# GroupNorm and self-attention block: rows of x load into the result's buffer, GpSimd adds the bias, and plain stores replace copies and accumulation

## The reference

```python
def _gn(v, G=32, eps=1e-5):
    g = v.reshape(B_, H_, W_, G, C_ // G)
    m = jnp.mean(g, axis=(1, 2, 4), keepdims=True)
    s = jnp.var(g, axis=(1, 2, 4), keepdims=True)
    return ((g - m) / jnp.sqrt(s + eps)).reshape(v.shape)

# inside _L0_conv_ref(inputs, Wq, bq, ...)
q = x @ Wq + bq
k = x @ Wk + bk
v = x @ Wv + bv
scores = jnp.einsum('bnc,bmc->bnm', q, k) * scale
attn = jax.nn.softmax(scores, axis=-1)
attended = jnp.einsum('bnm,bmc->bnc', attn, v)
out = attended @ Wo + bo

x = x + _L0_conv_ref(_gn(x), Wq, bq, Wk, bk, Wv, bv, Wo, bo)
```

## Time and profile before

| | before |
|---|---|
| median of three runs | 1805.6 us (1804.97 to 1805.94) |
| the profiled execution's own time | 1804.94 us |
| its span | 1803.3 us |
| TensorE (PE) busy | 1796.9 us, 100% |
| VectorE (DVE) busy | 1633.2 us, 91% |
| ScalarE (ACT) busy | 1056.0 us, 59% |
| GpSimd (POOL) busy | 91.1 us, 5% |
| DMA | 101.92 MB, mean 57 GB/s |
| granted TensorE clock | full, in every slice |

### The profile page before, as it was taken

How to read it: one execution, slowest core, us unless ns; L and a number is a source line. 1 busy time by engine, 2 the same in 40 slices (tenths; PEclk the granted TensorE clock), 3 DMA queues, 4 the chain that set the end, 5 groups by cost and what they waited for, 6 DMA issues and landing times.

```text
span 1803.3 us, 32710 instructions
## 1 busy us (share of the span) xinstructions
PE 1796.9 (100%) x11589; PEld 1642.3 (91%) x11589; DVE 1633.2 (91%) x2860; ACT 1056.0 (59%) x1417; POOL 91.1 (5%) x106
## 2 busy tenths in 40 slices
PE   9999999999999999999999999999999999999999
PEld 8989999899898999998999989999899898999989
DVE  7999899999998999989999999899998998999997
ACT  5565565665655656556565565565665656656563
POOL 0000000000000000000000000000000000000000
PEclk9999999999999999999999999999999999999999
DMA  3222122231222221322213232122221222311201
GB/s 117 59 70 66 23 62 58 70 70 37 44 60 68 70 52 29 69 59 70 58 23 70 58 70 63 21 67 58 70 70 34 47 59 69 70 47 34 68 14 36
DMA packets 28809, 101.92 MB, mean 57 GB/s; under 512 B 3189, under 2 KB 3962, under 8 KB 28794
## 3 DMA queue, kind: packets, MB, share of 16 engines
q0 software_dynamic: 9072, 33.03, 12.1%
q1 hardware_dynamic: 19722, 68.69, 11.4%
HBM read 68.16 MB, written 66.58 MB: 75 GB/s over the span
## 4 chain that ended last, share of the span: by engine, by line
PE 96%; DVE 2%; issue 1%; ACT 0%; POOL 0%; POOLq 0%; DVEq 0%; ACTq 0%
PE ps_s L861 47%; PE ps_o L955 13%; PE ps_o L956 13%; PE ps_o L957 13%; PE ps_o L861 9%; DVE s_buf L627 1%; PE ps_o L965 0%; DVE top L597 0%; DVE o_buf L647 0%; DVE query_max L614 0%; DVE h_lo L569 0%; ACT s_buf L347 0%; DVE top_turned L602 0%; DVE part_max L604 0%; DVE row_max L620 0%
## 5 line engine op out<-in xcount | busy, mean ns | idle before, releaser
L955 PE MATMUL ps_o<-v_rows,p_hi 128*128 128x258 f32 x2048 | 577.9, 282 | 0.0
L957 PE MATMUL ps_o<-v_rows,p_lo 128*128 128x258 f32 x2048 | 576.1, 281 | 0.0
L956 PE MATMUL ps_o<-v_lo,p_hi 128*128 128x256 f32 x2048 | 575.8, 281 | 0.0
L355 ACT ACTIVATE p_hi<-s_buf 128x1024 fp32r<-128x1024 f32 x256 | 272.3, 1064 | 439.1 <-DVE s_buf L627 439.1
L861 PE MATMUL ps_s<-g_hi,h_hi 128*128 128x512 f32 x1024 | 399.5, 390 | 1.1 <-DVE g_lo L577 0.9
L861 PE MATMUL ps_s<-g_hi,h_lo 128*128 128x512 f32 x1024 | 399.0, 390 | 0.0
L861 PE MATMUL ps_s<-g_lo,h_hi 128*128 128x512 f32 x1024 | 398.6, 389 | 0.0
L955 PEld LDWEIGHTS ps_o<-v_rows,p_hi 128*128 128x128 f32 x2048 | 385.9, 188 | 2.4
L956 PEld LDWEIGHTS ps_o<-v_lo,p_hi 128*128 128x128 f32 x2048 | 384.8, 188 | 2.9
L957 PEld LDWEIGHTS ps_o<-v_rows,p_lo 128*128 128x128 f32 x2048 | 384.6, 188 | 0.0
L347 ACT ACTIVATE s_buf<-ps_s 128x512 f32<-128x512 f32 x512 | 292.4, 605 | 136.3 <-PE ps_s L861 134.7
(11 more groups left out here) (95 smaller groups left out, 2229.3 us busy)
## 6 DMA issues: line engine op xcount, KB each, us to landing
x_t<-in_x_turned_dram SPq DMA_DIRECT2D x64, 512.0 KB, 3.9
out_dram<-in_x_dram SPq DMA_DIRECT2D x63, 512.0 KB, 7.1
out_dram<-o_buf POOLq DMA_DIRECT2D x63, 512.0 KB, 5.4
x_last<-in_x_dram SPq DMA_DIRECT2D x1, 512.0 KB, 7.6
out_dram<-o_buf SPq DMA_DIRECT2D x4, 128.0 KB, 2.0
s_buf<-in_L_conv_Wq_dram SPq DMA_DIRECT2D x1, 256.0 KB, 5.1
s_buf<-in_L_conv_Wk_dram SPq DMA_DIRECT2D x1, 256.0 KB, 5.3
s_buf<-in_L_conv_Wv_dram SPq DMA_DIRECT2D x1, 256.0 KB, 5.5
```

Of the source, the lines that this page charges most:

```text
L355: nc.scalar.activation(p_hi[c][:, rows, :], s_buf[c][:, rows, :], ACT.Exp, scale=SCALE).then_inc(p_hi_done, 1)
L955: nc.tensor.matmul(ps[:, 0:VC], p_hi[c][:, m, cols], v_hi[:, m, :], start=m == 0, stop=False)
L956: nc.tensor.matmul(ps[:, VC - C:VC], p_hi[c][:, m, cols], v_lo[:, m, :], start=False, stop=False)
L957: last = nc.tensor.matmul(ps[:, 0:VC], p_lo[c][:, m, cols], v_hi[:, m, :], start=False, stop=m == T - 1)
```

## The change

The rows of x are no longer copied from DRAM to DRAM. For each image and half they load into o_buf[c] itself. GpSimd adds out_bias to them in place, an instruction over 128x1024 with two inputs in SBUF. finish then adds the attend to what stands in o_buf[c], tile by tile, and SyncE stores the buffer with a plain transfer. As load and result share a buffer, a load waits for the store before it (stored), GpSimd for the load (rows_in), VectorE's first finish for GpSimd (rows_biased), and the store for the four finishes (o_out). The last image does the same, apart from the tile-by-tile stores at its end, which stay; x_last goes. weighed has a buffer of its own.

```diff
-        x_last = sb("x_last", [P, TQ, C])
+        weighed = sb("weighed", [P, C])[:]
...
-            def residual(b, c):
-
-                after(sp, x_copied[c], b * 16)
-                sp.dma_start(out_v[b, :, c * TQ:(c + 1) * TQ, :],
-                             x_v[b, :, c * TQ:(c + 1) * TQ, :]).then_inc(x_copied[c], 16)
+            def load_rows(b, c):
+                after(sp, stored[c], b * 16)
+                sp.dma_start(o_buf[c][:], x_v[b, :, c * TQ:(c + 1) * TQ, :]).then_inc(rows_in[c], 16)
+
+            def store(b, c):
+                sp.wait_ge(o_out, b * 8 + (4 * c + 4))
+                sp.dma_start(out_v[b, :, c * TQ:(c + 1) * TQ, :], o_buf[c][:]).then_inc(stored[c], 16)
...
             load_turned(1)
-            residual(0, 0)
-            residual(0, 1)
-            residual(1, 0)
-            residual(1, 1)
+            load_rows(0, 0)
+            load_rows(0, 1)
 
             def body(b):
                 load_turned(b + 1)
-                residual(b + 1, 0)
-                residual(b + 1, 1)
+                store(b - 1, 0)
+                load_rows(b, 0)
+                store(b - 1, 1)
+                load_rows(b, 1)
...
-            with sp.Fori(1, B - 2) as b:
+            with sp.Fori(1, B - 1) as b:
                 body(b)
-            load_turned(B - 1)
-            residual(B - 1, 0)
-            sp.dma_start(x_last[:], x_v[B - 1, :, TQ:2 * TQ, :]).then_inc(x_last_in, 16)
+            store(B - 2, 0)
+            load_rows(B - 1, 0)
+            store(B - 2, 1)
+            load_rows(B - 1, 1)
+            store(B - 1, 0)
             store_last_tiles()
...
-            def store(b, c):
-
-                after(pool, x_copied[c], b * 16 + 16)
-                after(pool, o_out, b * 8 + (4 * c + 4))
-                pool.dma_start(out_v[b, :, c * TQ:(c + 1) * TQ, :], o_buf[c][:],
-                               accum_op=ALU.add).then_inc(stored[c], 16)
+            def add_bias(b, c):
+                pool.wait_ge(rows_in[c], b * 16 + 16)
+                pool.tensor_tensor(o_buf[c][:], o_buf[c][:], out_bias[:].unsqueeze(1).broadcast_to([P, TQ, C]),
+                                   ALU.add).then_inc(rows_biased[c], 1)
...
             inverse_std(0)
             inverse_std(1)
-            store(0, 0)
+            pool.wait_ge(out_bias_done, 1)
+            add_bias(0, 0)
+            add_bias(0, 1)
             with pool.Fori(1, B - 1) as b:
-                store(b - 1, 1)
+                add_bias(b, 0)
                 inverse_std(b + 1)
-                store(b, 0)
-            store(B - 2, 1)
-            store(B - 1, 0)
+                add_bias(b, 1)
+            add_bias(B - 1, 0)
+            add_bias(B - 1, 1)
...
                 if j == 0:
-                    dve.wait_ge(out_bias_done, 1)
-                    after(dve, stored[c], b * 16)
+                    dve.wait_ge(rows_biased[c], b + 1)
...
-                                               in1=out_bias[:] if rows is None else rows, op0=ALU.mult, op1=ALU.add).then_inc(o_out, 1)
+                                               in1=o_buf[c][:, j, :], op0=ALU.mult, op1=ALU.add).then_inc(o_out, 1)
...
-                dve.wait_ge(x_last_in, 16)
-                nc.vector.tensor_tensor(x_last[:], x_last[:], out_bias[:].unsqueeze(1).broadcast_to([P, TQ, C]),
-                                        ALU.add).then_inc(x_last_done, 1)
```

More of the change, by code:

```diff
@@ L146, in attention_kernel @@
         bias_rows = tail[0:2 * K, 8 + C:8 + C + P]
-        weighed = o_buf[1][:, 0, :]
         wq_in = sem("wq_in")
@@ L154, in attention_kernel @@
         bias_turned = sem("bias_turned")
-        x_last_in = sem("x_last_in")
-        x_last_done = sem("x_last_done")
+        rows_in = [sem(f"rows_in{c}") for c in range(CH)]
+        rows_biased = [sem(f"rows_biased{c}") for c in range(CH)]
         last_stored = sem("last_stored")
@@ L168, in attention_kernel @@
         fold_done = sem("fold_done")
-        x_copied = [sem(f"x_copied{c}") for c in range(CH)]
         xt_landed = [sem(f"xt_landed{k}") for k in range(K)]
@@ L262, in store_last_tiles @@
                                  o_buf[1][:, j:j + 1, :]).then_inc(last_stored, 16)
-            with sp.Fori(1, B - 2) as b:
+            with sp.Fori(1, B - 1) as b:
                 body(b)
-            load_turned(B - 1)
-            residual(B - 1, 0)
-            sp.dma_start(x_last[:], x_v[B - 1, :, TQ:2 * TQ, :]).then_inc(x_last_in, 16)
+            store(B - 2, 0)
[3 more added lines that the diff above has]
+            store(B - 1, 0)
             store_last_tiles()
-            after(sp, x_copied[0], 16 * B)
-            after(sp, x_copied[1], 16 * (B - 1))
             sp.wait_ge(last_stored, 16 * TQ)
-            after(sp, stored[0], 16 * B)
-            after(sp, stored[1], 16 * (B - 1))
+            sp.wait_ge(stored[0], 16 * B)
+            sp.wait_ge(stored[1], 16 * (B - 1))
         @block.gpsimd
@@ L636, in p_rest, with finish @@
                                         ALU.subtract).then_inc(p_lo_done, 1)
-            def finish(b, c, j, rows=None):
+            def finish(b, c, j):
                 t = c * TQ + j
@@ L850, in _ @@
             last_image(B - 1)
-            dve.wait_ge(x_last_done, 1)
             for j in range(TQ):
-                finish(B - 1, 1, j, x_last[:, j, :])
+                finish(B - 1, 1, j)
         @block.tensor
```

## The result

The changed kernel took 1869.83 us (median of four runs, 1868.23 to 1870.21) against 1805.47 us: a ratio of 1.0355, 95% interval 1.0343 to 1.0367. It is slower by 64.4 us, where 26 were forecast and the range ended at 1852.

What follows compares the result with a forecast made beforehand. TensorE was taken as the bound, busy 1796.9 of 1803.3 us, with VectorE close behind. 24 us in the loop plus 2.3 at the start, on the median 1805.6, gave 1831.9, so 1832 us; range 1804 to 1852.

Steps and rivals of the forecast that it cites:

- What goes, and the new queues: Dropped copies, accumulating stores and x_last add, and the new store, load and waits on the queues: each worth 0.
- The 852.9 for the rows of half 0: Time in us when half 0's rows were expected in the buffer, after 4 us store and 4 us load.
- The add's length: GpSimd's add over 1024 elements with two inputs: taken as 2.3 us, between 1.6 and 3.1 us.
- Does it hold up VectorE: GpSimd's add was taken to hold VectorE's two-input instructions for its whole length, 2.3 us; chance of full hold-up 0.54.
- The case that an add yields to VectorE: Rival: no hold-up, nothing TensorE needs moves, 1805.6 us; chance 0.30, including a partial hold-up that slack absorbs.
- The rule that the second blocks until the first has ended: Skill's rule for VectorE and GpSimd on SBUF, used for the hold-up; by it the sum comes out at 1832 us.
- The second add: Half 1's add, behind inverse_std: makes the second g_lo 1.84 us late, TensorE waits 0.8 us an image, 30 times, 24 us.
- The threshold of 1.5 us: For the add behind inverse_std, TensorE's wait for g_lo is the add's length less 1.5 us.
- The first add: Half 0's add, at about 853: a maximum 2 us late, 0.7 us left after idling, v_lo has 1.7 us slack; cost 0.
- The row of 102.92: Profile row before the change: inverse_std took 1.94 us instead of 1.03 beside a two-input VectorE maximum; read as mutual exclusion.
- The start: Image 0: both adds right behind inverse_std(1), TensorE without slack for v_lo; 2.3 us, once.
- the end: Last image: the add falls beside a p_lo with about 1.3 us of slack; 0 to 0.3 us, taken as 0.

Runs made afterwards that it cites:

- the five reductions: Changed kernel plus five short VectorE reductions, results unused, between the variance and half 1's second maximum: 1851.03 us, ratio 1.0252.
- kernel with two short reductions: Changed kernel plus two short VectorE reductions, results unused, between the variance and half 1's second maximum: 1874.56 us, ratio 1.038.
- the doubled add: Changed kernel with only half 1's adds, each followed by a second same-size add on a scratch buffer; half 0 gets no bias: 1912.24 us, ratio 1.059.
- first run with placed adds: Changed kernel, half 0's add also waiting for its image's half 0 maxima, half 1's for the second h_lo: 1847.43 us, ratio 1.0233.

## Why the prediction was wrong

**What goes, and the new queues: right.** Both were put at 0; the change without the adds took the time of before. (The 852.9 for the rows of half 0 should be 844.6 + 8 = 852.6; nothing hangs on it.)

**The add's length: right.** 2.3 us was taken, 2.40 measured where nothing stands in its way.

**Does it hold up VectorE: right.** Taken from one row in the other direction and a rule; the stretched maxima of 3.10 and 2.65 us show it. The case that an add yields to VectorE (0.30) did not come. The Trainium skill, SBUF — State Buffer, section "Who interferes with whom", agrees on who is held: two SBUF inputs against GpSimd's reads, not against its writes, and COPY, which that section counts among those that can contend. The rule that the second blocks until the first has ended does not hold for a short read: the inverse_std of 883.32 came first and ran for 1.03 us, and the maximum of 883.35 lost nothing.

**The second add, 0.8 us an image: right in itself.** 0.86 and 0.88 us with this add alone, in the two kernels that tried it. The threshold of 1.5 us fits too: 1.4 us cost nothing, 2.4 us cost 0.86, two adds 2.85.

**The first add, cost 0: the step that failed.** The prediction said that VectorE idles after the hold, "which leaves about 0.7 us", and asked only whether the next v_lo would still be in time. It was. But it is not v_lo alone that has to be met. In the kernel before, VectorE waited 0.12 us for ScalarE, which is too short for a bracket in the rows, until just after inverse_std had begun: 883.32 against 883.35. That was a race won by 0.03 us. With what was left of the first hold the wait was gone, the maximum began first, and it held up inverse_std for 1.0 us in 28 images. The row of 102.92 had shown just this state; I read it as proof of the mechanism and not as a state that the change could make permanent. Alone, the first add and its lost race still fit into VectorE's waits, 0.16 us over.

**The slack was counted twice.** The step on the second add took VectorE to be on time when its turn came, and spent 1.04 us of slack there; the step on the first add spent the waits that would have made up that lateness in the next image. Over a full turn of the loop the check is this: before, an image had 4.86 us in which VectorE was not busy. After, it is busy 3.58 us longer and waits 1.0 us for inverse_std, and 57.73 - 54.44 = 3.29 us are left. Without that wait it is 2.3 us, small gaps between VectorE's own instructions and one wait of 0.24 us for ScalarE; with the five reductions, at another period, 57.09 - 54.80 is 2.3 us again. So VectorE's round, not one late instruction, sets the period.

**The sum.** With the second add alone an image takes 56.58 us; with both adds and the race won, 56.83 (one image of the changed kernel); with the race lost, 57.73. That is 0.86 for the second add, 0.25 for the first and 0.90 for the race, together 2.01, where 0.8 was forecast. The start was put at 2.3 us and came to 3.2, the end at 0 and came to 1.9.

What stays open: the exact split between the first add and the race. The one image with 56.83 rests on a VectorE that had just caught up; the wait of 0.98 us would leave a little less for the first add, and with the first add and its race alone the whole came to 0.16.

## What to carry to other kernels

Before work goes to GpSimd, look not at GpSimd's idle time but at what VectorE does in that stretch: in these runs two-input instructions and copies in SBUF stopped while an add read, statistics, reductions, a transpose and a finish went on, and a wait on the right semaphore moved the add among them for nothing in the loop. When a loop's slack is to pay for several delays, go once round the loop with all of them, and check at each short instruction of another engine who would come first if this engine were 0.1 us later. If a slow form of an instruction stands once in the profile of before, price it as if it stood in every pass.

## What the runs showed of the hardware

**A race decided within hundredths of a microsecond.** With the maximum 0.03 us behind, inverse_std kept its 1.03 us; with 0.02 us, it took 2.11 us; with 0.29 us, 1.02 us. The kernel with two short reductions shows both sides by itself: 0.02 us behind, 2.11 us; 0.04 us behind, 1.02 us. (The starts on GpSimd are themselves rough.)

**Two holds in a row.** GpSimd's adds back to back did not keep VectorE out for both: in the first image of the changed kernel the first two adds took 6.56 us together, and VectorE's maximum of 29.73 ran between them.

**TensorE's clock after a longer wait.** With the doubled add TensorE waits 2.36 us for g_lo in each image of the loop, as here:

```profile
246.28 0.49 PE L862 MATMUL ps_s<-g_hi,h_hi 128*128 128x512 f32 x1 [2.36 <-DVE g_lo L580]
```

In 9 of them what follows is what the windows above show: the granted clock falls from 1.00 to 0.50, the lower level of 1.2 GHz, for some 3.4 us, and the image takes 60.21 us instead of 58.57. At 9 times 1.64 us that is 15 us of the 107. The changed kernel has it once, behind its longest wait for g_lo, 2.1 us at 126.32, and not behind the 28 of 1.7 us:

```profile
106.15:164.97 58.82, 56.72 (x358) 51.32 (x357) 53.21 (x89) 32.73 (x44) 7.48 (x4) 0.97 0.15 54
```

The kernel with two short reductions has it in the loop six times, behind waits of 1.78 to 1.81 us, among 23 waits of 1.7 to 1.9 us. In the first run with placed adds, a wait of 2.36 us passed at the full clock. So the clock fell behind some waits of 1.8 to 2.4 us and stayed up behind others of the same length: the wait's length is not all that decides, and what else does stays open.
